# Scan rows stored as group, column pair, image instead of image, column pair

## What is computed

```python
def _row_conv(y, K):        # K: 9 taps, 64 channels in, 64 out
    return lax.conv_general_dilated(y, K, window_strides=(1,), padding=[(PW, PW)], ...)
def step(prev, cur):
    new = cur + jax.nn.relu(_row_conv(prev, K))
    return (new, new)
y = _dir_scan(y, k_td, reverse=False)      # rows, downwards
y = _dir_scan(y, k_dt, reverse=True)       # rows, upwards
yt = jnp.swapaxes(y, 1, 2)
yt = _dir_scan(yt, k_lr, reverse=False)    # columns
yt = _dir_scan(yt, k_rl, reverse=True)
```

## Time and profile before

| | us |
|---|---|
| runs | 665.71, 667.65, 667.8 (median 667.65) |
| span of the profiled execution | 664.7 |
| TensorE matmuls, busy | 632.9 (95%) |
| VectorE, busy | 568.4 (86%) |
| ScalarE, busy | 428.5 (64%) |
| GpSimd, busy | 128.2 (19%) |
| line 549 matmuls (the scans), busy | 421.4, 7560 of them, 219 ns each |

### The profile page before, as it was taken

One profiled execution on the slowest core, in us unless ns is written; L12 is line 12 of the kernel. 1 busy time (PEld: TensorE's weight loads), 2 busy tenths in 40 slices (PEclk: granted clock), 3 DMA queues, 4 the chain that ended last, 5 costly groups with the idle time before them and its releaser, 6 DMA issues.

```text
span 664.7 us, 27754 instructions
## 1 busy us (share of the span) xinstructions
PE 632.9 (95%) x10562; PEld 539.5 (81%) x10562; DVE 568.4 (86%) x1953; ACT 428.5 (64%) x1062; POOL 128.2 (19%) x112
## 2 busy tenths in 40 slices
PE   7799999999999999999999999998989999999991
PEld 5799999999999899999999999965646656655650
DVE  5689989999899888989999999989868778878784
ACT  3456666677777766666665666657666867867744
POOL 0022200000000000000000000000153666666654
PEclk9999999999999999999999999999999999999996
DMA  9999990233333100000000000000326368468546
GB/s 173 207 207 186 165 178 0 52 81 80 81 79 82 41 1 0 0 0 0 0 2 0 0 0 0 0 1 2 73 70 148 78 131 179 101 125 182 115 83 127
DMA packets 79314, 50.38 MB, mean 76 GB/s; under 512 B 44256, under 2 KB 72352, under 8 KB 79264
## 3 DMA queue, kind: packets, MB, share of 16 engines
q1 hardware_dynamic: 75936, 48.91, 36.6%
q10 hardware_dynamic: 3328, 0.82, 0.6%
HBM read 32.34 MB, written 9.24 MB: 63 GB/s over the span
## 4 chain that ended last, share of the span: by engine, by line
PE 49%; DVE 32%; issue 10%; ACT 3%; DMA 3%; DVEq 1%; POOL 1%; ACTq 0%; SPq 0%; POOLq 0%
PE bank L549 33%; DVE scan_rows L840 7%; DVE parts L813 7%; DVE parts L840 7%; PE bank L680 3%; DVE fin L927 2%; PE bank L630 2%; DVE rows_h L1004 2%; PE bank L616 2%; DVE stats L1045 2%; DVE kp L994 1%; PE bank L669 1%; PE bank L634 1%; PE bank L604 1%; DMA rows_h<-bounce 1%
## 5 line engine op out<-in xcount | busy, mean ns | idle before, releaser
L549 PE MATMUL bank<-parts 128*128 128x124 f16 (+2 forms) x7560 | 421.4, 219 | 7.5 <-issue 4.2
L549 PEld LDWEIGHTS bank<-parts 128*128 128x128 f16 x7560 | 415.4, 98 | 14.0 <-issue 5.7
L1222 ACT ACTIVATE parts<-parts 128x128 f16<-128x128 f16 x506 | 156.6, 310 | 150.0 <-DVE parts L840 125.1
L813 DVE TENSOR_TENSOR parts<-scan_rows,parts 128x128 f16<-128x128 f32 x506 | 148.9, 294 | 14.2
L840 DVE SCALAR_TENSOR_TENSOR parts<-bank,cols_w 128x128 f16<-128x128 f32 x378 | 109.5, 290 | 22.3 <-PE bank L549 7.1
L840 DVE SCALAR_TENSOR_TENSOR scan_rows<-bank,cols_w 128x128 f32<-128x128 f32 x378 | 105.9, 280 | 0.0
L442 POOL TENSOR_TENSOR scale<-dev,half 128x2 f32<-128x2 f32 (+1 forms) x2 | 2.1, 1036 | 401.5 <-DVE dev L952 401.5
L453 POOL TENSOR_TENSOR rows_h<-rows_h 128x512 f32<-128x512 f32 x52 | 67.9, 1339 | 47.3 <-DMA rows_h<-bounce 47.3
L994 DVE SCALAR_TENSOR_TENSOR kp<-ex,bank 128x512 f32<-128x512 f32 x64 | 40.8, 679 | 21.3 <-ACT ex L1355 20.9
L1233 ACT ACTIVATE cols_w<-scan_rows 128x256 f32 x126 | 52.5, 417 | 5.7 <-issue 0.2
L1361 ACT ACTIVATE ex<-bank,minus_one 128x512 f32<-128x512 f32 x64 | 40.6, 689 | 14.6 <-PE bank L616 14.6
(11 more groups left out here) (146 smaller groups left out, 591.6 us busy)
## 6 DMA issues: line engine op xcount, KB each, us to landing
rows_h<-bounce SPq DMA_DIRECT2D x52, 256.0 KB, 4.8
cols_w<-x SPq DMA_DIRECT2D x6, 896.0 KB, 12.0
ex<-scan_rows SPq DMA_DIRECT2D x84, 64.0 KB, 2.0
out<-fin SPq DMA_DIRECT2D x10, 512.0 KB, 7.3
cols_w<-x SPq DMA_DIRECT2D x12, 384.0 KB, 8.6
cols_w<-x SPq DMA_DIRECT2D x12, 256.0 KB, 6.3
cols_w<-x SPq DMA_DIRECT2D x6, 512.0 KB, 10.5
kp<-scan_rows SPq DMA_DIRECT2D x40, 64.0 KB, 1.9
```

The lines of the kernel that those rows point to most:

```text
L549: last = nc.tensor.matmul(conv_rows[g][u % SLOTS][:, :, to], w[:, k, d, :], rows_16[:, u % SLOTS, g * GB:(g + 1) * GB, of], start=part_n = ...
L813: nc.vector.tensor_tensor(low[:, slot, gb, :], state[:, slot, gb, :] if row is None else row[:, gb, :], high[:, slot, gb, :], ALU.subtract ...
L1222: act.activation(high_down[:, slot, gb, :], high[:, slot, gb, :], ACT.Copy, scale=1.0 / LOW_SCALE).then_inc(down_ready[g], 1)
```

## The change

All rows of the scan are stored as group, column pair, image: the 4 images of a group lie next to one another, and a tap's columns, being a range of column pairs, are one run. This holds for state, high, low and high_down, for rows_h, for the staging tiles of scan 1 (stage) and for the PSUM bank of each group. cols_w, raw and row0 keep their layout. So where `add` comes from raw or cols it is read in an order that is not the stored one (`by_column`), save to cols and the pieces of scan 1 write in such an order, and scan 1's `add` from rows_h is one run.

```diff
-        state = scan_rows[:, 0:SLOTS * ROW].rearrange("p (s b j) -> p s b j", s=SLOTS, b=B)
+        state = scan_rows[:, 0:SLOTS * ROW].rearrange("p (s g j b) -> p s g j b", s=SLOTS, g=GROUPS, j=J)
...
-                                .rearrange("p (s b j) -> p s b j", s=SLOTS, b=B) for n in range(3))
+                                .rearrange("p (s g j b) -> p s g j b", s=SLOTS, g=GROUPS, j=J) for n in range(3))
...
-        rows_h = sb("rows_h", [P, H, B, J])
+        rows_h = sb("rows_h", [P, H, GROUPS, J, GB])
...
-        conv_rows = [[c[:, 0:GB * J].rearrange("p (b j) -> p b j", b=GB) for c in conv[g]] for g in range(GROUPS)]
+        conv_rows = [[c[:, 0:GB * J].rearrange("p (j b) -> p j b", j=J) for c in conv[g]] for g in range(GROUPS)]
...
+        def by_column(row):
+            return row.rearrange("p b j -> p j b")
...
-                                    last = nc.tensor.matmul(conv_rows[g][u % SLOTS][:, :, to], w[:, k, d, :],
-                                                            rows_16[:, u % SLOTS, g * GB:(g + 1) * GB, of],
+                                    last = nc.tensor.matmul(conv_rows[g][u % SLOTS][:, to, :], w[:, k, d, :],
+                                                            rows_16[:, u % SLOTS, g, of, :],
...
-                                add = raw[:, u // RAW_ROWS, gb, 1 + r * W:1 + (r + 1) * W:2]
-                            elif k == 2:
-                                add = cols[:, bass.ds(s + (u + 1), 1), gb, :].rearrange("p o b j -> p (o b) j")
+                                add = by_column(raw[:, u // RAW_ROWS, gb, 1 + r * W:1 + (r + 1) * W:2])
+                            elif k == 1:
+                                add = rows_h[:, bass.ds(down - u, 1), g].rearrange("p o j b -> p (o j) b")
                             else:
-                                src = rows_h if k == 1 else cols
-                                add = src[:, bass.ds(down - u, 1), gb, :].rearrange("p o b j -> p (o b) j")
+                                add = by_column(cols[:, bass.ds(s + (u + 1) if k == 2 else down - u, 1), gb, :]
+                                                .rearrange("p o b j -> p (o b) j"))
...
-                gb = slice(g * GB, (g + 1) * GB)
-                return act.activation(pairs_of(cols_w[:, :], pw)[:, :, gb, bass.ds(jh, 1)]
-                                      .rearrange("p w b o -> p (o b) w"), stage[k % STAGES][:, pw, gb, :], ACT.Copy)
+                return act.activation(pairs_of(cols_w[:, :], pw)[:, :, g, :, bass.ds(jh, 1)]
+                                      .rearrange("p w b o -> p w (b o)"), stage[k % STAGES][:, pw, g], ACT.Copy)
...
-                        save((u + 1) % SLOTS, cols[:, bass.ds(w, 1), :, :].rearrange("p o b j -> p (o b) j"))
+                        save((u + 1) % SLOTS, cols[:, bass.ds(w, 1), :, :].rearrange("p o (g b) j -> p (o g) j b", g=GROUPS))
```

More of the change, by code:

```diff
@@ L119, in build @@
         row0 = scan_rows[:, SLOTS * ROW:].rearrange("p (b w) -> p b w", b=B)
-        flat_h = rows_h[:, :, :, :].rearrange("p h b j -> p (h b j)")
+        flat_h = rows_h[:, :, :, :, :].rearrange("p h g j b -> p (h g j b)")
         qp = flat_h[:, 0:2 * UNITS * CHUNK].rearrange("p (r u n) -> p r u n", r=2, u=UNITS)
@@ L131, in build @@
         fin = sb("fin", [P, J, W])
[L134 removed]
+        stage = [t[:, m, :].rearrange("p (w g j b) -> p w g j b", w=2, g=GROUPS, j=J)
                  for t, m in [(ex, m) for m in range(4)] + [(kp, m) for m in range(STAGES - 4)]]
@@ L809, in row_low_part @@
             def row_low_part(slot, g, rows, row=None):
-                gb = slice(g * GB, (g + 1) * GB)
                 dve.wait_ge(row_ready[g], rows)
-                nc.vector.tensor_tensor(low[:, slot, gb, :], state[:, slot, gb, :] if row is None else row[:, gb, :],
-                                        high[:, slot, gb, :], ALU.subtract).then_inc(low_ready[g], 1)
+                nc.vector.tensor_tensor(low[:, slot, g], state[:, slot, g] if row is None else row[:, g],
+                                        high[:, slot, g], ALU.subtract).then_inc(low_ready[g], 1)
             def last_columns(pw):
-                return cols_w[0:C, :].rearrange("p (w two b j) -> p w two b j", two=2, b=B, j=J)[:, :, pw, :, 0:1]\
-                    .rearrange("p w b o -> p (o b) w")
+                return cols_w[0:C, :].rearrange("p (w two g b j) -> p w two g b j", two=2, g=GROUPS, b=GB, j=J)[:, :, pw, :, :, 0]\
+                    .rearrange("p w g b -> p g w b")
             def last_step(g, rows, add):
                 nc.vector.scalar_tensor_tensor(
-                    out=state_4[:, PLACES - 1, g * GB:(g + 1) * GB, :],
-                    in0=conv[g][(STEPS - 1) % SLOTS][:, 0:GB * J].rearrange("p (b j) -> p b j", b=GB), scalar=0.0, in1=add,
+                    out=state_4[:, PLACES - 1, g], in0=conv_rows[g][(STEPS - 1) % SLOTS], scalar=0.0, in1=add,
                     op0=ALU.max, op1=ALU.add).then_inc(row_ready[g], 1)
             def start(g, rows, src):
-                gb = slice(g * GB, (g + 1) * GB)
-                nc.vector.tensor_copy(high[:, 0, gb, :], src).then_inc(high_ready[g], 1)
-                nc.vector.tensor_copy(state[:, 0, gb, :], src).then_inc(row_ready[g], 1)
+                nc.vector.tensor_copy(high[:, 0, g], src).then_inc(high_ready[g], 1)
+                nc.vector.tensor_copy(state[:, 0, g], src).then_inc(row_ready[g], 1)
                 row_low_part(0, g, rows)
@@ L836, in step @@
                 slot = (u + 1) % SLOTS
[L837 to L842, removed]
+                for to, ready in ((high[:, slot, g], high_ready), (state[:, slot, g] if row is None else row[:, g], row_ready)):
+                    nc.vector.scalar_tensor_tensor(out=to, in0=conv_rows[g][u % SLOTS], scalar=0.0, in1=add,
+                                                   op0=ALU.max, op1=ALU.add).then_inc(ready[g], 1)
                 beside(g)
@@ L849, in _ @@
             for g in range(GROUPS):
-                start(g, 1, row0[:, g * GB:(g + 1) * GB, 1:1 + W:2])
+                start(g, 1, by_column(row0[:, g * GB:(g + 1) * GB, 1:1 + W:2]))
             split_weights(dve, 0)
@@ L865, in _ @@
                     for g in range(GROUPS):
-                        start(g, rows, cols[:, 0, g * GB:(g + 1) * GB, :])
-                    nc.vector.tensor_copy(last_columns(1), state_4[C:P, PLACES - 1, :, :]).then_inc(last_odds_scattered, 1)
+                        start(g, rows, by_column(cols[:, 0, g * GB:(g + 1) * GB, :]))
+                    nc.vector.tensor_copy(last_columns(1), state_4[C:P, PLACES - 1]).then_inc(last_odds_scattered, 1)
                     dve.wait_ge(last_odds_scattered, 1)
@@ L1219, in down @@
                 for g in range(GROUPS):
-                    gb = slice(g * GB, (g + 1) * GB)
                     act.wait_ge(high_ready[g], n)
-                    act.activation(high_down[:, slot, gb, :], high[:, slot, gb, :], ACT.Copy,
+                    act.activation(high_down[:, slot, g], high[:, slot, g], ACT.Copy,
                                    scale=1.0 / LOW_SCALE).then_inc(down_ready[g], 1)
@@ L1232, in save @@
             def save(slot, to):
[L1233 removed]
+                act.activation(to, state[:, slot], ACT.Copy).then_inc(saved, 1)
             def pairs_of(t, pw):
[L1237 removed]
+                return t.rearrange("p (w two g b j) -> p w two g b j", two=2, g=GROUPS, b=GB, j=J)[:, :, pw]
             def scatter(pw, i):
                 ph = 1 - i % 2
[L1242 to L1244 removed]
+                return act.activation(pairs_of(cols_w[ph * C:(ph + 1) * C, :], pw)[:, :, :, :, 0]
+                                      .rearrange("p w g b -> p g w b"),
+                                      state_4[pw * C:(pw + 1) * C, i % PLACES], ACT.Copy)
             def piece(k, jh, pw, g):
[L1248 to L1250 removed]
+                return act.activation(pairs_of(cols_w[:, :], pw)[:, :, g, :, bass.ds(jh, 1)]
+                                      .rearrange("p w b o -> p w (b o)"), stage[k % STAGES][:, pw, g], ACT.Copy)
             def rows_moved(n, i):
@@ L1270, in _ @@
                     down((u + 1) % SLOTS, s + (u + 2))
-                    save((u + 1) % SLOTS, rows_h[:, bass.ds(s + (u + 1), 1), :, :].rearrange("p o b j -> p (o b) j"))
+                    save((u + 1) % SLOTS, rows_h[:, bass.ds(s + (u + 1), 1)].rearrange("p o g j b -> p (o g) j b"))
             for i in range(1, 4):
```

4 lines of the change are left out of this document (2 added, 2 removed).

## The result

The kernel after takes 708.51 us (median; 707.58, 708.42, 708.61 and 709.94 in four runs), the one before 667.72 in the same comparison: a ratio of 1.061, interval 1.059 to 1.063. It is 6.1% slower; the forecast was 709 us.

What follows compares the result with a forecast made beforehand. TensorE bounds the kernel, VectorE close behind and equal in scan 3. Span 664.7 + 44.5 (reads) - 2 (stalls) - 1.3 (taps) = 705.9, plus 2.95 around it: 709 us; own range 697 to 732, 8 in 10 from 664 to 736.

Steps and rivals of the forecast that it cites:

- The read by column: VectorE's line 840, scans 0, 2 and 3: 85 ns more per instruction of 128 elements, four per step, 340 ns.
- The margin of VectorE: Scans 0 and 2: VectorE needs 1.50 us per step against TensorE's 1.64; becomes 1.84, adding 25.2 us.
- Scan 3: VectorE has no room in about 48 steps with statistics: 16.3 us more, plus 3.0 us in the other 15.
- Taps: TensorE, all scans: 124-column taps in one run save 20 ns per step; scan 1 gains 1.3 us.
- The save: ScalarE, scans 2 and 3: 638 ns when writing 128 bytes apart, delay mostly covered, taken at nothing.
- Rival B: VectorE's reads free, ScalarE's save delays scans 2 and 3 by 0.02 to 0.05 us per step: 668.5 us, chance 0.14.
- Stalls of scan 0: Scan 0's stalls leave VectorE idle anyway and the slower pace covers part of them: 2 us taken off.
- A: VectorE's reads by column are free and the kernel gets faster: 663.5 us, chance 0.20.
- C: VectorE's reads by column cost a full doubling, 130 ns each, in scans 0, 2 and 3: 743 us, chance 0.12.
- D: VectorE's reads by column cost a partial 40 ns each in scans 0, 2 and 3: 677 us, chance 0.10.
- E: TensorE: all off-centre taps gain from one run, 84 ns per step, with free reads: 652 us, chance 0.02.

Runs made afterwards that it cites:

- e5: Kernel before, old layout and taps kept, but input row read by column in scans 0, 2 and 3 (wrong pixels); 711.23 us, ratio 1.062.
- e1: Kernel after, but input row read in stored order in scans 0, 2 and 3 (wrong pixels), scattered save kept; 663.13 us, ratio 0.992.
- e6: Kernel after, but only the float32 output reads the input row by column; the float16 output reads in stored order (wrong pixels); 681.35 us, ratio 1.018.
- v1: Full computation, against the kernel before: only float16 parts and PSUM stored by column pair, everything float32 by image; 708.62 us, ratio 1.060.
- e4: Kernel before, input row read in 8-, 16- and 12-byte steps and pairs 16 bytes apart in scans 0 to 3 (wrong pixels); 681.54 us.
- e7: Kernel before, but the two inner taps cut to 30 column pairs, in four runs of even length with even starts; 659.21 us.
- e9: Kernel after with read and save in stored order, and all off-centre taps over 30 column pairs in one run of 120; 660.86 us.
- e2: Kernel after, but the save of scans 2 and 3 writes one run (wrong places), read by column kept; 707.81 us, ratio 1.059.
- e3: Kernel after with both read and save in stored order (wrong pixels), leaving only the taps in one run; 664.48 us, ratio 0.995.
- v2: Full computation, kernel before with the layout by column in scan 1 alone, scan 0's save turning the row; 665.73 us, ratio 0.997.
- e8: Kernel before, but the two inner taps cut to 30 column pairs, in four runs of even length with one odd start; 667.36 us.

## Why the prediction was right

The direction, the place and the size were right, and the runs show the mechanism: e5 has the loss with the read alone, e1 is without it once the read is put back, and e6, with half of the reads, has 38% of it, counted from e1.

- **The read by column.** Taken at 85 ns from line 1192, measured 80 and 84 ns. The nearest row was one of a jumping write, and that it fitted is partly luck: v1 shows that a stepped write and a jumping read need not cost the same. e4 shows which reads pay.
- **The margin of VectorE.** 1.50 us was taken in scans 0 and 2. Scan 0 came to 1.798 against 1.84 forecast, since the chain needs 1.47 when it is never held up and such a read 80 ns; scan 2 came to 1.884 against 1.84, since about 80 ns more stand in one of its two turns, by the traces the register arithmetic. I had carried scan 0's cycle over to scan 2 without looking at its timeline. The two errors cancel: forecast 25.2 us less 2, measured 8.1 + 14.9 = 23.0.
- **Scan 3.** 1.98 forecast in the steps with statistics, 1.95 measured in them, and 1.79 in those of the first loop block, without statistics, where 1.84 was forecast; 19.3 us against 17.6.
- **Taps.** 20 ns a step forecast, 25 measured in scan 1 (1.640 to 1.615); 1.3 us against 0.7 in this profile, and 1.6 in e1's. The odd runs are the cause of 20 of the 25, by e7 to e9.
- **The save.** 638 ns taken, 662 measured, and taken as hidden: e2 gives 14 ns in scan 2 and none in scan 3. Here is ScalarE in scan 2 of the kernel after:

```profile
301.00 0.31 ACT L1219 ACTIVATE parts<-parts 128x128 f16<-128x128 f16 x1 [0.58 <-DVE parts L839]
301.44 0.68 ACT L1230 ACTIVATE cols_w<-scan_rows 128x256 f32 x1
302.00 0.31 ACT L1219 ACTIVATE parts<-parts 128x128 f16<-128x128 f16 x1
```

The save that starts at 301.44 is followed by the next down at 302.00, which comes 0.43 us after the start of its float16 output (301.57 in the timeline above), an output of 0.39 us: the down starts hardly later than its input is ready. Rival B, which gave the save 20 to 50 ns a step if reads were free, is refuted by e1: with free reads and a long save scans 2 and 3 are below 1.64.
- **Stalls of scan 0.** 2 us were taken off. The steps over 1.15 times the median exceed it by 7.8 us before and 6.5 after, so about 1.3 us were covered.

The rivals fall thus: A's and B's premise, a free read, is false (e5); C's 130 ns and D's 40 ns are not met; E is refuted by e7 and e9, which are equal. What stays open is how the price of a stepped float16 write depends on the step, what SBUF and PSUM each take of an odd run, and what holds scan 2 at 1.63 us in e1 and e3.

## What to carry to other kernels

When a layout is turned to suit one engine, list the streams of every other instruction that touches it: here 25 ns a step were won on TensorE and 160 to 310 lost on VectorE, which had only 0.14 us behind TensorE. VectorE's float32 read from SBUF kept its full rate here as long as it took two elements in a row from each 16 bytes (8-byte steps, or pairs 16 bytes apart). It is the next engine's whole cycle, added up from starts in the timeline, not from the lengths of records, and in every loop by itself, that tells what such a read may cost. Turn a layout only in the stretch in which all streams become one run, as v2 does, and let an engine with room do the turning at its border.

## What the runs showed of the hardware that I had not expected

- A float16 output of VectorE written in 8-byte steps makes the record of 128 elements some 160 ns longer (v1: 490 against 320 to 330 ns; 452 against 294 where a float16 input is stepped too), but the next instruction starts only about 40 ns later. A float32 read of 128 elements in jumps delays the next one by its whole 80 ns (0.29 us from high to state in scan 0 after, 0.21 before).
- VectorE reading PSUM in 16-byte steps costs 40 ns for 128 elements (v1: 320 against 280), half as much as in SBUF.
- Matmuls with runs of even length and odd start are as slow as with two columns more in each run (e8 1.635 against e7 1.595 us a step).
- ScalarE's save slows from 417 to 662 ns with writes 128 bytes apart and to 671 in v2 with writes 16 bytes apart, 0.96 and 0.99 ns an element, more than the 0.86 that line 1242 had shown.
